# Layer-1 attention scores from f32 q and k held in 32-row lanes, their maxima turned in f32 and added to q, in place of bf16 parts stacked through DRAM

## The chip, the cores and the metric

The kernel runs on one core of one Trainium2 chip, as one program. The metric is the device time of one execution in microseconds (us); the median of three executions of the kernel before is 785.51 us (784.35 to 786.27). Five engines work in parallel, each through its own instructions in order: PE (matrix products), DVE (vector), ACT (scalar functions and copies), POOL (here memsets and indirect gathers) and SP (it issues DMA transfers). Engines wait for one another by semaphores. PE writes to PSUM banks of 512 f32 columns, from which DVE and ACT read.

## What is computed

Two transformer layers over x of 4 batches x 256 tokens x 256 values, each layer LayerNorm, attention, a gate, and `x + s * g`:

```
xn = layernorm(x)
s  = attention0(xn)      # 32 heads of 8 values, 8 k/v heads, biases, no mask
g  = silu(experts(xn))   # W_up, W_down, 45 keys, top 8 of 64 pairs, 8 heads x 8 experts a token:
                         # gathered rows of down_embed and up_embed
x  = x + s * g
xn = layernorm(x)
s  = attention1(xn):
       q = (xn @ Wq)                       # 16 heads of 16
       k, v = split(xn @ Wkv)              # 4 heads of 16, q head h reads k head h % 4
       scores = q k^T / sqrt(16) + slope[h] * (key - query)   for key <= query, else -inf
       out = softmax(scores) @ v, then @ Wo + bo
g  = silu(int8_linear(xn))                 # q = round(xn / scale), q @ weight^T, scales, bias, f16
x  = x + s * g
```

Layer 0 feeds layer 1 within a batch; batches are independent.

## The kernel before, in words

A batch is 256 tokens, two tiles of 128 rows. What a batch does is cut into stages, each with a number of calls: `stage:b.n` is call n of batch b. The order of the calls on each engine is written out by hand in four tables, `PE_PLAN` (L76), `ACT_PLAN` (L122), `DVE_PLAN` (L156) and `SP_PLAN` (L196); four batches are interleaved in them. A call waits by semaphores for what it reads and for what it overwrites; a wait at the head of an engine holds up all calls behind it.

**The experts of layer 0** run over 64 groups g (16 a batch), each for one head of 128 tokens. POOL gathers 8 x 128 table rows of 384 values a group (L551, one indirect DMA per expert, 512 in all) into one of `RING` = 4 slots. DVE's `dots:g` multiplies the first 128 values of each row with the token's h (L1204), ACT's `tanh` and DVE's `zs` (L1214) make the factors, ACT's `diag` (L1049) writes three of them on diagonals, DVE's `acc:g` (L1229) sums five of the eight rows and PE's `add:g` (L831) sums the other three into the PSUM bank `experts`. POOL may gather group g when `add` and `acc` of group g-4 are done. After the eight groups of a tile DVE's `mix` (L1290, L1292) joins both sums and frees `experts` for the next tile; add:16, add:24, ... add:48 are the first adds after a mix.

**Attention 0 and, before the change, attention 1** get f32 accuracy from bf16 products: DVE's `split` (L1174 to L1176) cuts q and k into three bf16 parts, SP stores the parts to DRAM (`store_parts`, L490, L491) and loads them back stacked (`load_stack`, L503, L506), so that one product of up to 128 rows holds all pairs of parts (`stackq`, `stackk`). `max0` and `max1` (L683; L696, L698, L701) are scores with the queries in rows, of which DVE takes the negated row maxima; `nm0`, `nm1` split the maxima in three and bring them as rows to `stackq` (layer 0) or `slopeq` (layer 1: transposed at L711, copied by ACT, placed by a DMA). `sc0` and `sc1` (L734; L743, L744, L746) are the scores again with the keys in rows, less the maxima; ACT takes their exponent (L997) and `pv0`, `pv1` (L766, L777) multiply with v. In layer 1 a unit of `max1` or `sc1` is four heads of one k head (`quad_of`): 12 units a batch, of which 8 lie on the diagonal and take a mask product (below, near units) and 4 do not (far). The ALiBi term is a product of its own, `slopeq` x `slopek`, of 512 bf16 columns. Then `ctx1` transposes the context, `over1` on DVE divides by the sums, `flip1` and `proj1` (L571, L807, L811) transpose and multiply with Wo. `turnq` and `quant` (L674) are the int8 linear layer.

**qkv1** (L629 to L641) makes q (256 columns twice), k and v from `x1T`, whose transposes (L571) ACT copies out; ACT copies q and k twice, in f32 and in bf16. PSUM banks of the stages' results are three, used in turn (`TURNS` = 3), in the order in which PE's plan names them. `warm:0.0` and `warm:0.1` (L839), at the end of PE's plan, are products whose results nobody reads.

**The start.** POOL clears the upper rows of `stackk` and `stackq`, then v0 and v1, and writes ones into v (L533 to L540). DVE normalises batch 0 (L1067 to L1080), PE transposes it (L571, with `ident`) and so on, until the first 128 lookups of batch 0 are there and POOL gathers.

A record of the trace is one pass of PE: a plain f32 product leaves two records (x2), a bf16 product or a transposition one. `order` listings, below, count products.

## Time and profile before

| | before |
|---|---|
| median of 3 executions | 785.51 us (784.35 to 786.27) |
| the profiled execution | 787.66 us |
| its span in the trace | 785.8 us |
| granted TensorE clock, mean | 0.823 |
| PE busy | 528.0 us (67%) |
| DVE busy | 592.4 us (75%) |
| ACT busy | 255.8 us (33%) |
| POOL busy | 514.9 us (66%), of which 512 gathers 505.0 us |

The span is from the first instruction to the last in the trace; 1.9 us of the profiled execution lie around it. POOL's gathers take 986 ns each with 0.30 us between two of them. PE's clock is 2.4 GHz where the trace shows 1.00 and 1.2 GHz where it shows 0.5; a value in between is a stretch with both. "Idle" at an instruction is the time in which its engine did nothing before it, and the arrow names who ended that.

### The profile page before, as it was taken

How to read it: one execution, taken by the hardware profiler on the slowest of the kernel's cores; microseconds unless marked ns; L12 is line 12 of the kernel's file. 1: busy time of each engine (PE TensorE's matmuls, PEld its weight loads, DVE VectorE, ACT ScalarE, POOL GpSimd, SP SyncE). 2: the span in 40 equal slices, each digit the busy share in tenths (PEclk: the TensorE clock that was granted, in tenths of full speed). 3: DMA queues.
4: the chain of work that ended last, by engine and by line, in shares of the span. 5: the costliest groups of instructions: out<-in, count | busy, mean ns of one | idle time of the engine just before them, and what ended most of it. 6: DMA issues, size and time to landing. Idle time of an engine off the chain costs nothing.

```text
span 785.8 us, 9193 instructions
## 1 busy us (share of the span) xinstructions
PE 528.0 (67%) x2241; PEld 291.8 (37%) x2258; DVE 592.4 (75%) x2700; ACT 255.8 (33%) x648; POOL 514.9 (66%) x522
## 2 busy tenths in 40 slices
PE   2810466486794567797758558956356996979786
PEld 2600254232373235334336235324233443354432
DVE  4487977797874987799779788869799875775351
ACT  1600151144541112463424114623111473425032
POOL 5077777777775777777777777777777777760000
PEclk9955787788986666899868767978777998989898
DMA  8157565555575555955765555596865559550400
GB/s 292 38 165 220 168 173 155 154 156 155 151 223 162 156 156 165 232 153 153 210 198 159 156 158 160 158 237 186 210 191 153 154 153 256 157 142 1 106 2 15
DMA packets 47765, 125.49 MB, mean 160 GB/s; under 512 B 10715, under 2 KB 20507, under 8 KB 46654
## 3 DMA queue, kind: packets, MB, share of 16 engines
q0 software_dynamic: 32768, 100.70, 45.3%
q1 hardware_dynamic: 14342, 23.90, 10.9%
q10 hardware_dynamic: 600, 0.30, 0.2%
q8 instruction: 18, 0.29, 0.2%
q14 instruction: 37, 0.30, 0.1%
HBM read 119.58 MB, written 4.98 MB: 159 GB/s over the span
## 4 chain that ended last, share of the span: by engine, by line
POOL 50%; issue 18%; PE 13%; DVE 12%; DMA 5%; ACT 1%; POOLq 0%; ACTq 0%; DVEq 0%
POOL rows L551 50%; DMA rows<-experts_table,idx 5%; PE experts L831 3%; DVE hot L1204 3%; DVE acc L1229 2%; PE outs L777 1%; PE experts L839 1%; PE turn L586 1%; PE turn L811 1%; DVE nmax L1245 1%; DVE nmax L1237 1%; PE scores L743 1%; DVE bestp L1129 1%; DVE var L1072 1%; PE turn L807 1%
## 5 line engine op out<-in xcount | busy, mean ns | idle before, releaser
L551 POOL DMA_INDIRECT rows<-experts_table,idx x512 | 505.0, 986 | 188.7 <-issue 151.4
L1204 DVE CUSTOM_DVE_ANT_0 hot<-rows,h 128x128 f32<-128x128 f32 x512 | 114.6, 287 | 108.6 <-DMA rows<-experts_table,idx 108.4
L831 PE MATMUL experts<-rows,diag 128*128 128x256 f32 x384 | 132.4, 497 | 45.4 <-ACT diag L1049 38.2
L683 PE MATMUL turn<-stackk,stackq 125*128 125x256 bf16 x256 | 58.4, 344 | 105.8 <-DVE nmax L1237 52.1
L1229 DVE SCALAR_TENSOR_TENSOR acc<-rows,zs,acc 128x256 f32<-128x256 f32 x304 | 125.7, 478 | 0.9 <-issue 0.3
L831 PEld LDWEIGHTS experts<-rows,diag 128*128 128x128 f32 x384 | 93.3, 254 | 76.5 <-ACT diag L1049 47.0
L997 ACT ACTIVATE probs<-scores 128x512 f32<-128x512 f32 x176 | 97.3, 594 | 59.6 <-PE scores L734 31.1
L1043 ACT ACTIVATE zt<-za 128x8 f32<-128x8 f32 x64 | 13.4, 209 | 259.5 <-DVE za L1208 259.3
L1049 ACT ACTIVATE diag<-ident,zs 128x128 f32<-128x128 f32 x192 | 63.1, 394 | 68.3 <-DVE zs L1214 63.8
L1237 DVE TENSOR_REDUCE nmax<-turn 128x2 f32<-128x512 f32 x128 | 82.2, 682 | 1.8 <-PE turn L683 1.7
L683 PEld LDWEIGHTS turn<-stackk,stackq 125*128 125x128 bf16 x256 | 21.7, 111 | 143.8 <-DVE nmax L1237 78.5
L766 PE MATMUL outs<-probs,v 128*32 128x512 f32 x256 | 68.0, 624 | 7.6 <-ACT probs L997 7.2
L734 PE MATMUL scores<-stackq,stackk 128*128 128x512 bf16 x113 | 38.2, 402 | 8.8 <-DMA stackq<-nmaxT 4.1
L1204 DVE DVE_READ_ACCUMULATOR2_ANT z<- 128x1 f32 x512 | 41.4, 81 | 0.0
L586 PE MATMUL turn<-xnT,wup 128*128 128x256 f32 x128 | 36.0, 443 | 3.1 <-DVE nmax L1237 2.3
L586 PEld LDWEIGHTS turn<-xnT,wup 128*128 128x128 f32 x128 | 28.6, 228 | 9.9 <-DVE nmax L1237 1.9
L734 PEld LDWEIGHTS scores<-stackq,stackk 128*128 128x128 bf16 x128 | 9.9, 101 | 56.8 <-ACT probs L997 31.8
L696 PE MATMUL turn<-slopeq,slopek 128*128 128x512 bf16 x48 | 19.5, 407 | 15.1 <-DMA stackk<-scratchk 9.9
L777 PE MATMUL outs<-probs,v 128*32 128x512 f32 x96 | 25.4, 619 | 1.7 <-ACT probs L997 1.7
L1245 DVE TENSOR_REDUCE nmax<-turn 128x4 f32<-128x512 f32 x32 | 20.9, 683 | 5.5 <-PE turn L701 5.5
L615 PE MATMUL turn<-simw,h2T 128*128 128x360 f32 x32 | 16.9, 656 | 10.5 <-ACT sims L865 9.0
L571 PE MATMUL turn<-ident,th_up 128*128 128x128 f32 x16 | 4.4, 430 | 27.5 <-DVE th_up L1080 16.8
(156 smaller groups left out, 751.5 us busy)
## 6 DMA issues: line engine op xcount, KB each, us to landing
rows<-experts_table,idx POOLq DMA_INDIRECT x512, 3.2
stackq<-scratchq SPq DMA_DIRECT2D x20, 384.0 KB
scratchq<-parts SPq DMA_DIRECT2D x8, 384.0 KB, 3.2
stackk<-scratchk SPq DMA_DIRECT2D x20, 96.0 KB
xnext<-x SPq DMA_DIRECT2D x4, 256.0 KB, 3.2
wup<-w_wup SPq DMA_DIRECT2D x1, 1024.0 KB, 4.9
slopeq<-c_slopeq SPq DMA_DIRECT2D x1, 1024.0 KB, 5.2
xres<-x SPq DMA_DIRECT2D x4, 256.0 KB, 3.4
```

Source lines behind the costliest of these rows:

```text
L551: nc.gpsimd.indirect_dma_start(rows[:, slot, c, :], None, tab, bass.IndirectOffsetOnAxis(ap=idx[:, b % 2, t, TOP * h + c:TOP * h + c + 1], ...
L586: ins = mm(ps[:, a * S:(a + 1) * S], wup[:, c, (2 * j + a) * P:(2 * j + a + 1) * P], xnT[:, c, :], start=(c == 0), stop=(c == DC - 1))
L683: ins = mm(ps[:, t * S:(t + 1) * S], stackq[0][r, m, t * P:(t + 1) * P], stackk[0][r, m // QUAD, :], start=True, stop=True)
L734: mm(scores[:, score_bank(0, UNITS[0] * b + m), :], stackk[0][:, u, kc * P:(kc + 1) * P], stackq[0][:, hd:hd + 2, :], start=True, stop=Tru ...
L766: ins = mm(outs[WIN * strip:WIN * (strip + 1), :], v0[:, kc, lead:lead + WIN], probs[:, nth[0, UNITS[0] * b + AT_ONCE * n + i] % PROBS, :] ...
L777: ins = mm(outs[WIN * u:WIN * (u + 1), :], v1[:, tk, WIN * u:WIN * (u + 1)], probs[:, nth[1, UNITS[1] * b + AT_ONCE * n + i] % PROBS, :], ...
L831: ins = mm(experts[:, s // FH, :], diag[:, g % 2, k, :], rows[:, g % RING, k, PRIV:ROW], start=(s % FH == 0 and k == 0), stop=(s % FH == F ...
L997: fn(probs[:, at % PROBS, :], scores[:, at % SCORES, :], ACT.Exp).then_inc(exp_done[layer], 1)
L1049: ins = fn(diag[:, g % 2, k, :], ident[:, :], ACT.Copy, scale=zs[:, g % FACTORS, k:k + 1])
L1204: ins = v.tensor_tensor_reduce(out=zjunk[:, k, :], in0=rows[:, slot, k, 0:PRIV], in1=h2[:, b % 2, t, :], scale=1.0, scalar=0.0, op0=ALU.mu ...
L1229: ins = v.scalar_tensor_tensor(total, row, factor, total, ALU.mult, ALU.add)
L1237: v.tensor_reduce(nmax[0][:, :, m], ps[:, :].rearrange("p (t k) -> p t k", k=S), AX.X, ALU.max, negate=True)\
```

## The change

Layer 1 keeps q and k in f32. The 128 rows of `q1` (128 x 4 x 256) and `k1` (128 x 256) are four lanes of 32 rows, one for each k head: row 0 of a lane is 1 in k, row 1 holds the slope in q and the key position in k, rows 2 to 17 the head's 16 values (slope x query is the same for all keys of a query and is left out). `wq1` and `wk1` are padded to this layout by the host. Part by part:

- `qkv1` is three calls with a bank each: k and v (with a bf16 product `rowk` x `posk` that writes ones and positions into k, L654), then q in two halves, each 4 f32 products of 256 columns (L661): 8 for q where there were 4. ACT copies k and v, and q with the slopes as bias; no bf16 copies.
- `max1` is, for a near unit, a bf16 mask product (L700) and four f32 products of one lane (32 rows) with 128 columns each (L703); a far unit has the four alone. Before: bf16 512 columns, 4 x 128 columns, and the mask's 512.
- `sc1` is the mask product (near, L751) and one f32 product of a lane with 512 columns (L752). Before: bf16 512 columns twice, and the mask's 512.
- The maxima of `max1` go to row 0 of each lane in `nwide` (128 x 2 x 4 x 128 f32). `nm1:b.t` on PE transposes four 128 x 128 blocks of it into a bank (L723), and the new `lift1:b.t` on DVE adds the bank to a half of `q1`. Gone: `split_maxima` of layer 1, ACT's copy and DMA.
- Gone with the parts: `split1` on DVE, `store1` and `stack1` on SP (8 transfers a batch), the loads of `slopeq` (1 MB) and `slopek`, and both calls of `warm`.
- POOL clears v0, v1 and `nwide` first and the stacks after `xn0_ready`, that is when DVE has normalised batch 0; SP's `ones:0.0` waits for that.
- The tables are written anew. The plan's calls around the last batch of layer 0 and at the end are among those that moved.

```diff
-    qkv0:3.0 max1:1.5 ctx0:2.0 add:0.46 flip0:2.0 add:0.47 proj0:2.0 max1:1.6 max1:1.7 max0:3.0 max0:3.1 add:0.48 add:0.49
...
+    sc1:1.4 sc1:1.5 sc1:1.6 max0:3.0 max0:3.1 max0:3.2 sc1:1.7 pv1:1.2 sc1:1.8 pv1:1.3 max0:3.3 max0:3.4 max0:3.5 sc1:1.9
+    add:0.48 add:0.49 max0:3.6 max0:3.7 max0:3.8 pv1:1.4 add:0.50 max0:3.9 sc1:1.10 max0:3.10 sc1:1.11 max0:3.11 pv1:1.5
...
-        slopeq = sb("slopeq", [P, H1, S], BF16)
-        slopek = sb("slopek", [P, 2, S], BF16)
+        slopes = sb("slopes", [P, QUAD])
+        rowk = sb("rowk", [P, P], BF16)
+        posk = sb("posk", [P, S], BF16)
...
+        q1 = sb("q1", [P, QUAD, S])
+        k1 = sb("k1", [P, S])
...
+        nwide = sb("nwide", [P, TT, QUAD, P])
+        nlanes = nwide[:, :, :, :].rearrange("p t j (u r) -> p t j u r", r=LANE)
...
-            nc.gpsimd.memset(stackk[0][CLEARED_FROM:P, :, :], 0.0)
-            nc.gpsimd.memset(stackq[0][CLEARED_FROM:P, :, :], 0.0).then_inc(cleared, 1)
-            pool.wait_ge(cleared, 1)
             nc.gpsimd.memset(full(v0), 0.0)
             nc.gpsimd.memset(full(v1), 0.0).then_inc(cleared, 1)
+            pool.wait_ge(cleared, 1)
+            nc.gpsimd.memset(v0one, 1.0)
+            nc.gpsimd.memset(v1one, 1.0)
+            nc.gpsimd.memset(full(nwide), 0.0).then_inc(cleared, 1)
             pool.wait_ge(cleared, 2)
-            nc.gpsimd.memset(v0one, 1.0)
-            nc.gpsimd.memset(v1one, 1.0).then_inc(cleared, 1)
+            pool.wait_ge(xn0_ready, 1)
+            nc.gpsimd.memset(stackk[CLEARED_FROM:P, :, :], 0.0)
+            nc.gpsimd.memset(stackq[CLEARED_FROM:P, :, :], 0.0).then_inc(stacks_cleared, 1)
...
+            def qkv1(b, n):
+
+                if b == 0 and n == 0:
                     pe.wait_ge(late_in, LATE_IN)
                 pe.wait_ge(drained["norm1"], b + 1)
-                qkv("qkv1", b, wq1, wk1, wv1, None, x1T)
+                ps = bank("qkv1", 3 * b + n)
+                if n == 0:
+                    mm(ps[:, 0:S], full(rowk), full(posk), start=True, stop=False)
+                    for c in range(DC):
+                        mm(ps[:, 0:S], wk1[:, c, :], x1T[:, c, :], start=False, stop=(c == DC - 1))
+                    ins = values_of(ps, wv1, x1T, None)
+                else:
+                    for a in range(2):
+                        for c in range(DC):
+                            ins = mm(ps[:, a * S:(a + 1) * S], wq1[:, c, 2 * (n - 1) + a, :], x1T[:, c, :],
+                                     start=(c == 0), stop=(c == DC - 1))
+                ins.then_inc(filled["qkv1"], 1)
...
             def max1(b, m):
                 if m == 0:
                     if b == 0:
-                        pe.wait_ge(late_in, LATE_IN)
                         pe.wait_ge(halves, 2)
-                    pe.wait_ge(stack_in[1], STACK_IN[1] * (b + 1))
+                    pe.wait_ge(drained["qkv1"], 3 * (b + 1))
                 u, tq, tk = quad_of(m)
                 ps, q, k = bank("max1", UNITS[1] * b + m), slice(tq * P, (tq + 1) * P), slice(tk * P, (tk + 1) * P)
-                each = ps[:, :].rearrange("p (j k) -> p j k", k=P)
-                mm(each, slopek[:, 0, q], slopeq[:, QUAD * u:QUAD * (u + 1), k], start=True, stop=False)
+                near = tq == tk
+                if near:
+                    mm(ps[:, :].rearrange("p (j k) -> p j k", k=P), full(identb),
+                       maskb[:, :].unsqueeze(1).broadcast_to([P, QUAD, P]), start=True, stop=False)
                 for j in range(QUAD):
-                    ins = mm(ps[:, j * P:(j + 1) * P], stackq[1][:, QUAD * u + j, q], stackk[1][:, u, k], start=False,
-                             stop=tq != tk and j == QUAD - 1)
-                if tq == tk:
-                    ins = mm(each, full(identb), maskb[:, :].unsqueeze(1).broadcast_to([P, QUAD, P]), start=False, stop=True)
+                    ins = mm(ps[:, j * P:(j + 1) * P], q1[lane(u), j, q], k1[lane(u), k], start=not near,
+                             stop=not near or j == QUAD - 1)
                 ins.then_inc(filled["max1"], 1)
...
+            def nm1(b, t):
+                if t == 0:
+                    pe.wait_ge(drained["max1"], UNITS[1] * b + QUADS[1])
+                else:
+                    pe.wait_ge(nmax1_ready, b + 1)
+                ps = bank("nm1", TT * b + t)
+                for j in range(QUAD):
+                    ins = tr(ps[:, j * P:(j + 1) * P], nwide[:, t, j, :], full(ident))
+                ins.then_inc(filled["nm1"], 1)
...
             def sc1(b, m):
-                if m == 0:
-                    pe.wait_ge(nmax_in[1], 16 * (b + 1))
                 u, tq, tk = quad_of(m)
-                q, k, hd = slice(tq * P, (tq + 1) * P), slice(tk * P, (tk + 1) * P), slice(QUAD * u, QUAD * (u + 1))
+                if m in (0, QUADS[1]):
+                    pe.wait_ge(drained["nm1"], TT * b + tq + 1)
+                q, k = slice(tq * P, (tq + 1) * P), slice(tk * P, (tk + 1) * P)
                 to = scores[:, score_bank(1, UNITS[1] * b + m), :].rearrange("p (j q) -> p j q", q=P)
-                mm(to, slopek[:, 1, k], slopeq[:, hd, q], start=True, stop=False)
-                ins = mm(to, stackk[1][:, u, k], stackq[1][:, hd, q], start=False, stop=tq != tk)
-                if tq == tk:
-                    ins = mm(to, full(identb), maskT[:, :].unsqueeze(1).broadcast_to([P, QUAD, P]), start=False, stop=True)
-                ins.then_inc(scores_ready[1], 1)
+                near = tq == tk
+                if near:
+                    mm(to, full(identb), maskT[:, :].unsqueeze(1).broadcast_to([P, QUAD, P]), start=True, stop=False)
+                mm(to, k1[lane(u), k], q1[lane(u), :, q], start=not near, stop=True).then_inc(scores_ready[1], 1)
...
+            def qkv1(b, n):
+                ps = bank("qkv1", 3 * b + n)
+                if n == 0:
+                    wait_from(act, scores_ready[1], UNITS[1] * b)
+                    wait_from(act, pv_done[1], PRODUCTS[1] * b)
+                    fn(full(k1), ps[:, 0:S], ACT.Copy)
+                    ins = fn(v1at, ps[:, S:S + TT * VD].rearrange("p (t g d) -> p t g d", t=TT, d=HD1), ACT.Copy)
+                else:
+                    if b == 0:
+                        act.wait_ge(late_in, LATE_IN)
+                    for a in range(2):
+                        j = 2 * (n - 1) + a
+                        ins = fn(q1[:, j, :], ps[:, a * S:(a + 1) * S], ACT.Identity, bias=slopes[:, j:j + 1], scale=HD1 ** -0.5)
+                ins.then_inc(drained["qkv1"], 1)
...
             def max1(b, m):
                 u, tq, tk = quad_of(m)
+                wait_from(dve, filled["nm1"], TT * (b - 1) + tq + 1 if b else 0)
                 dve.wait_ge(filled["max1"], UNITS[1] * b + m + 1)
-                ps, hd = turn[turns.bank["max1", UNITS[1] * b + m]], slice(QUAD * u, QUAD * (u + 1))
-                to = nmaxd[:, hd] if tk else nmax[1][:, tq, hd]
+                ps = turn[turns.bank["max1", UNITS[1] * b + m]]
+                to = nmaxd[:, :, u] if tk else nlanes[:, tq, :, u, 0]
...
             def nm1(b, _):
-                split_maxima(1, b)
+                dve.wait_ge(drained["max1"], UNITS[1] * (b + 1))
+                v.tensor_tensor(nlanes[:, 1, :, :, 0], nlanes[:, 1, :, :, 0], full(nmaxd), ALU.min).then_inc(nmax1_ready, 1)
+
+            def lift1(b, t):
+
+                dve.wait_ge(filled["nm1"], TT * b + t + 1)
+                dve.wait_ge(filled["max1"], UNITS[1] * b + (QUADS[1] if t == 0 else UNITS[1]))
+                ps = turn[turns.bank["nm1", TT * b + t]]
+                to = q1[:, :, t * P:(t + 1) * P]
+                v.tensor_tensor(to, to, ps[:, :].rearrange("p (j q) -> p j q", q=P), ALU.add).then_inc(drained["nm1"], 1)
```

The tables' two pieces above are of PE's plan, where before `add:48` follows the first two `max0` of batch 3, and after it comes after six of them. In the order of the instructions as built, three places:

**POOL from its first own instruction to the gathers**, before and after (v is v0, then v1; the names with few columns write the ones):

```order
L533 MEMSET stackk 64x2048
L534 MEMSET stackq 64x8192
L536 MEMSET v 128x576
L537 MEMSET v 128x256
L539 MEMSET v 128x2x8
L540 MEMSET v 128x8
L551 DMA rows<-experts_table,idx 128x384 x512
```

```order
L522 MEMSET v 128x576
L523 MEMSET v 128x256
L525 MEMSET v 128x2x8
L526 MEMSET v 128x8
L527 MEMSET nwide 128x1024
L530 MEMSET stackk 64x2048
L531 MEMSET stackq 64x8192
L542 DMA rows<-experts_table,idx 128x384 x512
```

The two stack memsets moved from the head to a place behind v, `nwide` and the wait for the normalised batch 0, just ahead of the gathers.

**PE around add:48 and add:49 (L831 before, L836 after), where batch 3 of layer 0 meets batch 1 of layer 1.** L683 and L687 are `max0:3`, two products a head; L811 projects; L751 and L752 are `sc1:1`, L782 `pv1:1`; L696 to L701 `max1:1`. Before, then after:

```order
L811 MATMUL turn<-wo,headsT 128x256 x4
L696 MATMUL turn<-slopeq,slopek 128x512
L698 MATMUL turn<-stackk,stackq 128x128 x4
L701 MATMUL turn<-maskb,identb 128x512
L696 MATMUL turn<-slopeq,slopek 128x512
L698 MATMUL turn<-stackk,stackq 128x128 x4
L701 MATMUL turn<-maskb,identb 128x512
L683 MATMUL turn<-stackk,stackq 128x256 x4
L831 MATMUL experts<-rows,diag 128x256 x6
L683 MATMUL turn<-stackk,stackq 128x256 x12
L831 MATMUL experts<-rows,diag 128x256 x3
```

```order
L752 MATMUL scores<-q,k 128x512 x2
L751 MATMUL scores<-maskT,identb 128x512
L752 MATMUL scores<-q,k 128x512
L687 MATMUL turn<-stackk,stackq 128x256 x6
L751 MATMUL scores<-maskT,identb 128x512
L752 MATMUL scores<-q,k 128x512
L782 MATMUL outs<-probs,v 32x512 x2
L752 MATMUL scores<-q,k 128x512
L782 MATMUL outs<-probs,v 32x512 x2
L687 MATMUL turn<-stackk,stackq 128x256 x6
L752 MATMUL scores<-q,k 128x512
L836 MATMUL experts<-rows,diag 128x256 x6
```

Where two heads of `max0:3` and two units of `max1:1` stood ahead of add:48, there are now `sc1:1.4` to `sc1:1.9`, `max0:3.0` to `3.5` and `pv1:1.2`, `1.3`; `max1:1` is over by then. The first product of batch 3's stack is L683 before and L687 after.

**PE from the last layer norm to the first scores of batch 3 of layer 1.** Before, then after:

```order
L571 MATMUL turn<-ident,qf 128x128 x4
L777 MATMUL outs<-probs,v 32x512 x2
L629 MATMUL turn<-headsT,wq 128x256 x4
L634 MATMUL turn<-headsT,wk 128x256 x2
L641 MATMUL turn<-wv,headsT 128x64 x4
L788 MATMUL turn<-ident,ctxT 128x128 x8
L571 MATMUL turn<-ident,heads 128x128 x4
L807 MATMUL turn<-bo,ident 128x512
L811 MATMUL turn<-wo,headsT 128x256 x4
L839 MATMUL experts<-stackk,identb 128x512 x28
L696 MATMUL turn<-slopeq,slopek 128x512
L698 MATMUL turn<-stackk,stackq 128x128 x4
```

```order
L836 MATMUL experts<-rows,diag 128x256 x3
L812 MATMUL turn<-bo,ident 128x512
L816 MATMUL turn<-wo,headsT 128x256 x4
L562 MATMUL turn<-ident,qf 128x128 x4
L654 MATMUL turn<-posk,rowk 128x256
L656 MATMUL turn<-headsT,wk 128x256 x2
L624 MATMUL turn<-wv,headsT 128x64 x4
L661 MATMUL turn<-headsT,wq 128x256 x8
L562 MATMUL turn<-identb,qb 128x128 x4
L700 MATMUL turn<-maskb,identb 128x512
L703 MATMUL turn<-k,q 128x128 x4
```

The projection of batch 2 (L807, L811; after L812, L816) moved ahead of the transposes of batch 3's normalised rows (L571 and L562 from `qf`), the warm-up products (L839) are gone, and `max1:3` (after L700, L703) follows `qkv1:3` and `turnq:3` directly.

## Rows read from the trace of the kernel before

**Rows 1.** The page: the chain that ended last, shares of the span.

```profile
POOL 50%; issue 18%; PE 13%; DVE 12%; DMA 5%; ACT 1%; POOLq 0%; ACTq 0%; DVEq 0%
```

**Rows 2.** Who waited for whom, POOL: us in total, times, longest.

```profile
POOL rows L551 <- PE experts L831: 8.1, 9, 5.7
```

**Rows 3.** Order of time to 40 us: start, us, instruction, [idle before <-releaser].

```profile
2.48 6.92 POOL L534 MEMSET stackq<- 64x8192 bf16 x1
...
4.39 5.04 DVE L1072 TENSOR_SCALAR var<-mv 128x2 f32<-128x2 f32 x1
...
8.16 0.21 ACT L870 ACTIVATE bup_half<-bup 128x8 f32<-128x8 f32 x1 [6.13 <-DMA bup<-w_bup]
...
9.46 0.59 POOL L536 MEMSET v<- 128x576 f32 x1
...
10.36 0.18 DVE L1074 TENSOR_SCALAR rstd<-bits 128x2 int32<-128x2 uint32 x1
...
13.22 1.09 PE L571 MATMUL turn<-ident,th_up 128*128 128x128 f32 x4 [13.22 <-DVE th_up L1080]
...
38.15 1.09 POOL L551 DMA_INDIRECT rows<-experts_table,idx  x1 [27.63 <-DVE idx L1160]
```

**Rows 4.** Order of time around group 20, DVE and POOL.

```profile
244.02 0.29 DVE L1204 CUSTOM_DVE_ANT_0 hot<-rows,h 128x128 f32<-128x128 f32 x1 [9.20 <-DMA rows<-experts_table,idx]
...
250.06 1.14 POOL L551 DMA_INDIRECT rows<-experts_table,idx  x1 [5.66 <-PE experts L831]
```

**Rows 5.** Order of time, 499 to 581 us, PE, DVE and POOL.

```profile
499.08 1.46 PE L831 MATMUL experts<-rows,diag 128*128 128x256 f32 x6
...
540.16 1.00 PE L641 MATMUL turn<-wv,xnT 128*128 128x64 f32 x8
...
545.63 0.96 DVE L1176 TENSOR_TENSOR parts<-hot,parts 128x768 bf16<-128x768 f32 x1
...
570.24 1.04 PE L683 MATMUL turn<-stackk,stackq 125*128 125x256 bf16 x4 [11.60 <-DMA stackk<-scratchk]
...
574.94 5.18 PE L831 MATMUL experts<-rows,diag 128*128 128x256 f32 x12 [3.67 <-DVE mixed L1292]
...
580.26 1.04 POOL L551 DMA_INDIRECT rows<-experts_table,idx  x1 [0.30 <-PE experts L831]
```

**Rows 6.** Windows: length, busy of PE PEld DVE ACT POOL, clock, DMA.

```profile
500.00:541.00 41.00, 30.91 (x140) 14.97 (x140) 31.65 (x155) 15.06 (x37) 31.49 (x32) 0.88 0.75 203
...
664.00:701.00 37.00, 29.78 (x159) 15.33 (x162) 29.33 (x122) 15.90 (x38) 28.20 (x29) 0.92 0.60 179
...
730.00:737.00 7.00, 5.65 (x13) 3.73 (x14) 1.11 (x3) 0.60 (x1) 0.00 (x0) 0.52 0.74 165
```

**Rows 7.** DVE in order of time, then the chain after the last gather.

```profile
719.37 0.73 DVE L1080 TENSOR_SCALAR qf<-x,mv,rstd 128x256 f32<-128x256 f32 x2
...
724.15 0.86 PE turn L634 x4
...
737.45 5.99 PE experts L839 x27
...
743.44 0.22 PE turn L696
...
744.13 1.35 DVE nmax L1245 x2
...
762.41 0.98 PE outs L777 x4
...
763.39 0.32 PE scores L743
...
772.97 0.61 ACT ctxT L1010
```

**Rows 8.** Order of time, PE: an f32 product of 128 columns, then of 64.

```profile
34.76 0.38 PE L636 MATMUL turn<-bv,ident 128*128 128x128 f32 x2
...
34.98 1.00 PE L641 MATMUL turn<-wv,xnT 128*128 128x64 f32 x8
```

464 lines of the change are left out of this document (200 added, 264 removed).

## The prediction

> **What bounds the kernel now.** First the page's chain of what ended last: half of the span is POOL's gathers, and the 18% "issue" is mostly the 0.30 us between two of them [rows 1]. So from 38.15 us, when the first gather starts, to 706 us the time is 512 gathers, and a change elsewhere counts there only by what it lets POOL wait. The view of who waited for whom says how much that is: 8.1 us behind PE's adds in nine waits, the longest 5.7 [rows 2]. The rest of the span is a start, in which POOL waits 27.6 us for the first indices [rows 3], and a tail after the last gather, where PE, DVE and ACT take turns. I read three stretches closely.
>
> At the start DVE's `var`, two columns, takes 5.04 us where the like `rstd` takes 0.18, and it ends when POOL's 6.92 us memset of `stackq` ends; PE's first transposes wait for DVE at 13.22 [rows 3]. Before group 20 POOL idles 5.66 us behind PE's add, which follows a mix on DVE that stands behind rows awaited until 244.02 [rows 4]. Around 540 to 580 layer 0's last batch is stacked: `qkv0:3` ends at 541.0 on PE, the split on DVE ends at 546.6, the first `max0:3` starts at 570.24 when the stack has landed, add:48 and add:49 follow at 574.94, and POOL goes on at 580.26 with no more than its normal gap [rows 5]. There the adds' lead over POOL is 580.26 - 577.5, the end of add:48, the latter 2.6 us (half of 5.18) after its start: 2.8 us of slack.
>
> **Part 1, the start: -5.0.** The stack memsets leave the head of POOL, and v with 576 columns costs 0.59 [rows 3], so `nwide` with 1024 costs 1.0 by columns: POOL is done with what is left at about 3, ahead of DVE's 4.39. DVE then gets back 4.9 on `var` and 0.7 on `bits`, and the first transposes start at 7.6. PE next needs other loads: the last small one of those for `up`, `bup`, is there by 8.16 [rows 3], and the transposes and their copy (13.22 to 15.0) end at 9.4, after that. I take 5.0 of 5.6, leaving 0.6 for weights that may now be late. Bounds: 0, if another cause held DVE, and 5.6. The memsets of the stacks now run beside PE's `up`, 8.7 us before `split0:0`. They are ahead of the gathers on POOL, but those wait for indices much longer.
>
> **Prices of the lane products.** The trace has no product of 32 rows. What it has, by columns, at full clock: an f32 product of 128 columns 0.22 (34.76 to 34.98) [rows 8], of 256 columns 0.43 (two in 0.86), thus of 512 0.86; a bf16 one of 512 columns 0.22 [rows 7]. I take the lane products at these, the nearest rows there are. For a change between a lane and the whole array I take the nearest rows, `pv`, whose products go to strips of 32 columns: four records cost 0.98 where 4 x 0.22 = 0.88 is the columns' time, and the scores after them 0.32 instead of 0.22 [rows 7]: 0.10 + 0.12, about 0.2 for a round trip. Bounds: 0 and 0.4. Only near units switch (mask, whole array, then lanes). So a near unit of `max1` is 0.22 + 4 x 0.22 + 0.2 = 1.3, a far one 0.9; `sc1` near 0.22 + 0.86 + 0.2 = 1.3, far 0.9. A batch: `max1` 8 x 1.32 + 4 x 0.9 = 14.2, `sc1` 13.9. Before, by the 0.22 a record set, these were 7.0 and 6.9. `qkv1` adds four products of q (1.7), less the leaner rest; `nm1` adds six transposes, 1. PE gains some 17 us of work a batch, and POOL-bound time pays for it only where PE's slack ends.
>
> A record here lasts 0.38 where the next starts 0.22 after it (34.76 to 34.98 [rows 8]); were PE emptied at each change, both ways would cost 2 x 0.16 = 0.32 instead of 0.2. That is rival (c) below. The Trainium skill, TensorEngine Tiling (Array Packing), section Key Properties, says that changing the tiling mode drains TensorE; that speaks against this change, which makes 16 such round trips a batch, and by it the sum would be 783.9 and not 780.7. The strips of `pv`, at 0.2, agree only in part.
>
> **Part 2, group 20: 0.** The new order has the same calls (dots:18 ahead of the mix) on DVE, so the stall of 5.66 stays [rows 4].
>
> **Part 3, batch 3's stack: +3.5.** This is where slack was least. From 500 to 541 PE was busy 30.9 of 41 us at clock 0.88 [rows 6]. The new plan puts between the end of add:42 and that of `qkv0:3`: 11 pairs of `pv` (10.8), 20 `sc0` with their switches (5.5), all 12 `max1:1` (14.2), `nm1` (1.3), 3 adds (3.9), `sc1:1.0` to `1.3` (5.2), `turnq` (0.3), `qkv0:3` (3.9): 45 us. add:42 starts at 499.08 [rows 5] and ends at 500.4; 2 us later now, as `qkv1:1` with more products stands right ahead. 502.4 + 45.3 = 547.7 (all in the old time scale, the -5.0 apart) for 541.0. DVE's split follows at once now, without the 2.9 us of other work ahead of it, and ends at 551.7 for 546.6. Store and stack took 23.6 from there (546.6 to 570.24), so `max0:3` starts at 575.3. Ahead of add:48 stand now six `max0`, three units of `sc1` and two pairs of `pv`, 6.4 us against 4.7 before. add:48 ends at 575.3 + 6.4 + 2.6 = 584.3, against 580.3 where POOL would go on: 3.5 to 4, of which later groups give back nothing, since POOL has no slack of its own. Bounds: 0, if PE kept the old pace, to 8, where the work is 0.1 dearer a lane product.
>
> **Part 4, the end: -3.3.** From 664 to 701 PE was busy 29.8 of 37 us [rows 6]; with `max1:2`, `sc1:2` and more it is full in groups 58 to 62, and I put add:62 and `ctx1` about 3 us late. DVE's last norm, which needs the last mix, ends at 722.1 for 720.1 [rows 7]: +2.0, as the last projections now stand ahead in PE's plan but off this path. From there to the end before took 65.7. Now: transposes and copy 1.8; `qkv1:3` with eight q products 5.7; last copy 0.75; `max1`, `sc1` and the rest of the block 36.8, which is 14.2 + 13.9, three pairs of `pv` twice (5.9), `nm1` 1.3, `quant` 0.6, and 0.9 of waiting for a lift. DVE needs 0.68 a unit (1.35 for two [rows 7]), under PE's 0.9 and 1.3. The last part from ctxT at 772.97 [rows 7] to 785.8 stays, 12.85. PE idles 3.8 us during the norm; before, an idle stretch of that length at 726.7 to 730.6 was followed by 7 us at clock 0.52 [rows 6], the lower of its two levels. This time the 7 us hold `qkv1` and the first `max1`: I put 2.5 on it, below the 3.5 that half the clock costs on constant work. Sum 60.4, for 65.7: -5.3, and +2.0 makes -3.3. What goes is the DVE split, store and stack, which 27 warm-up records (5.99 us of 737.45 on [rows 7]) filled in. Bounds: -8, if switches and clock cost nothing and the norm ends on time; +4, at dearer products and a full half-clock price.
>
> **Sum.** 785.8 - 5.0 + 3.5 - 3.3 = 781.0 of span, 782.9 for the profiled execution (787.66 before), which lay 2.15 above the median. Median 785.51 - 4.8 = 780.7. A measurement of this kernel can tell from no change about 0.3%, 2.4 us.
>
> **The rivals.** (a) Lanes are cheap: no cost of switching, PE keeps pace, no stall at 52, the end on time. For it: rows of a product that are unused cost nothing elsewhere. Then -5.0, 0 and -7.7: 772.8. (b) Slower: the weights of a lane do not load behind the product before. 48 products of `max1` a batch are 128 columns behind a new load each; at 0.32 for 0.22, each batch's `max1` costs 4.8 more in three places where PE is by then the bound: the stall at 52 becomes 8.3, the end +3, the tail +4.8: 780.7 + 12.6 = 793.3. For it: four products of 64 columns cost about 0.84 (1.00 less the last record's 0.16 over its spacing), 0.21 each and not 0.11 [rows 8]: new weights set their pace, and 128 columns only just cover them. Against it: they do cover them. It decides from 0.26 us a product, where 780.7 becomes 785.7. (c) Full drains: 0.32 a round trip, 16 in the tail (+1.9) and 11 in part 3 (+1.3): 783.9. (d) Half clock more often: each switch leaves idle pieces, and PE drops to 1.2 GHz as in 730 to 737 in one or two busy stretches; six us each of doubled work, half hidden: 786.5. (e) Neighbouring lanes side by side: products of two lanes overlap. Only far units stand next to a unit of another lane, which saves 1.8 in the tail and 1 in part 3: 777.5.
>
> On (e), the trace has no two products in different rows at one time. The Trainium skill, same page and section, says that tiles operate independently and can run in parallel; by it the whole of lanes back to back would overlap, which the plan offers only between far units.
>
> (f) The change does not do what it says at the start: DVE was held by something other than the memset, and 5.0 is not gained: 785.7.
>
> **How the numbers follow.** Forecast 780.7: 0.38. (a) 772.8: 0.20. (b) 793.3: 0.14. (c) 783.9: 0.08. (d) 786.5: 0.06. (e) 777.5: 0.06. (f) 785.7: 0.08. Low 771 takes in (a) with 2 us, high 790 takes in (c), (d), (f) and the lesser half of (b): about 0.8 within, with what lies beyond (a). Faster by over 2.4 us: the forecast's case, (a) and (e): 0.64. Slower by over 2.4: (b): 0.14. Within 2.4: (c), (d) and (f): 0.22.
>
> **What would show it.** Start: `var` at 0.2 us and the first gather at 33 to 33.5. Prices: `max1`'s f32 products 0.22 us apart, near units 1.3 in the block. Batch 3: `qkv0:3` ending about 1.7 later than before in absolute time (547.7 - 5.0), and POOL idle 3 to 4 us once at group 52; none if (a). End: norm's last row 60 us ahead of the end, and clock 0.5 for 7 us right behind it. I would be wrong if lane products take 0.26 us or more, if PE's backlog reaches the adds of other groups (add:24 to add:40 have some slack that I did not go through one by one), or if the start waits on a load instead.

## The result and the profile after

The changed kernel takes 807.76 us (median of 4, 806.58 to 813.05), the kernel before 785.26 in the same set; the ratio is 1.0287, 95% interval 1.0257 to 1.0316. The forecast was 780.7, in a range of 771 to 790: it was wrong, in sign too. The profiled execution took 806.58 with a span of 804.7 (before 787.66 and 785.8), so 18.9 us of span have to be found.

The start, answering [rows 3], from the timelines of DVE, PE and POOL after:

```profile
4.80 0.17 DVE L1058 TENSOR_SCALAR var<-mv 128x2 f32<-128x2 f32 x1
...
8.85 1.12 PE L562 MATMUL turn<-ident,th_up 128*128 128x128 f32 x4 [8.85 <-DMA bup<-w_bup]
...
34.05 1.09 POOL L542 DMA_INDIRECT rows<-experts_table,idx  x1 [17.35 <-DVE idx L1146]
```

DVE's `var` is fast, the first gather is 4.1 us earlier, and the limit is now the load of `bup`. The gather stream, from who waited for whom on POOL, and the middle, from the timelines, answering [rows 2, 5]:

```profile
POOL rows L542 <- PE experts L836: 16.9, 7, 9.2
```

```profile
565.88 1.03 PE L687 MATMUL turn<-stackk,stackq 125*128 125x256 bf16 x4 [7.96 <-DMA stackk<-scratchk]
568.40 0.61 PE L687 MATMUL turn<-stackk,stackq 125*128 125x256 bf16 x2 [1.49 <-ACT proj L858]
568.89 0.61 PE L751 MATMUL scores<-maskT,identb 128*128 128x512 bf16 x1
569.42 2.07 PE L752 MATMUL scores<-q,k 32*128 32x512 f32 x2
571.43 1.92 PE L782 MATMUL outs<-probs,v 128*32 128x512 f32 x4
...
579.92 2.86 PE L836 MATMUL experts<-rows,diag 128*128 128x256 f32 x12
...
581.76 0.98 POOL L542 DMA_INDIRECT rows<-experts_table,idx  x1 [9.16 <-PE experts L836]
```

Every PE row from 568.40 to 577 lasts about twice what its like lasts elsewhere: `pv` 1.92 for 1.05, a lane product with 512 columns 2.07 for 1.12. The stream from first to last gather takes 668.7 us for 665.1: 9.7 more of waits for PE and DVE, 5.8 less of gathers (975 ns for 986).

The tail, windows of the kernel after: length, busy time of PE, PEld (TensorE's weight loads), DVE, ACT, POOL, granted clock, DMA share and GB/s. It answers [rows 6, 7]:

```profile
718.00:740.00 22.00, 16.51 (x75) 12.85 (x74) 11.56 (x35) 3.73 (x9) 0.00 (x0) 0.84 0.04 13
740.00:760.00 20.00, 20.00 (x83) 14.35 (x82) 6.23 (x9) 1.19 (x2) 0.00 (x0) 0.50 0.00 0
760.00:770.00 10.00, 10.00 (x28) 3.64 (x27) 2.32 (x5) 1.79 (x3) 0.00 (x0) 0.50 0.01 2
770.00:780.00 10.00, 9.22 (x23) 2.40 (x20) 1.51 (x3) 3.39 (x6) 0.00 (x0) 0.67 0.00 0
780.00:790.00 10.00, 10.00 (x16) 1.94 (x16) 0.00 (x0) 1.79 (x3) 0.00 (x0) 0.50 0.00 1
```

This is the finding. From 740 to 770 PE is busy in 30.00 of 30.00 us, and its granted clock is 0.50 throughout, the lower of its two levels. Before, 27 whole-array products and the block after them ran at 1.00, though PE was busy for less of the time:

```profile
744.00:773.00 29.00, 25.97 (x150) 10.62 (x149) 12.22 (x27) 9.78 (x18) 0.00 (x0) 1.00 0.01 2
```

PE's timeline after shows the fall, and it is not at an idle stretch:

```profile
737.43 0.39 PE L700 MATMUL turn<-maskb,identb 128*128 128x512 bf16 x1
737.75 1.15 PE L703 MATMUL turn<-k,q 32*128 32x128 f32 x8
738.83 0.39 PE L700 MATMUL turn<-maskb,identb 128*128 128x512 bf16 x1
739.15 1.61 PE L703 MATMUL turn<-k,q 32*128 32x128 f32 x8
740.70 0.61 PE L700 MATMUL turn<-maskb,identb 128*128 128x512 bf16 x1
741.23 4.11 PE L703 MATMUL turn<-k,q 32*128 32x128 f32 x24
745.27 1.11 PE L723 MATMUL turn<-ident,nwide 128*128 128x128 f32 x4
746.18 0.63 PE L700 MATMUL turn<-maskb,identb 128*128 128x512 bf16 x1
746.75 2.07 PE L703 MATMUL turn<-k,q 32*128 32x128 f32 x8
748.75 0.61 PE L700 MATMUL turn<-maskb,identb 128*128 128x512 bf16 x1
```

Four products of a lane (8 records) cost 1.08 (737.75 to 738.83) before the fall and 2.00 (746.75 to 748.75) after it. PE idled nowhere between 736.02, where it had waited 0.71 us for ACT, and the fall at about 740. The clock came back once, at about 770, behind the int8 products, eight records of `pv1` and four transpositions, and fell again within 4 us in lane products of `sc1`:

```profile
770.38 0.66 PE L723 MATMUL turn<-ident,nwide 128*128 128x128 f32 x4
771.82 1.13 PE L752 MATMUL scores<-q,k 32*128 32x512 f32 x4 [0.78 <-DVE q L1248]
...
775.16 2.07 PE L752 MATMUL scores<-q,k 32*128 32x512 f32 x2
```

**Where the 18.9 us are**, by spans: first gather -4.1; stream +3.6; last gather to the end of the last norm (725.04 for 720.10) +5.4; from there to the end 79.7 for 65.7, +14.0. I call the stretch from the first `max1:3` (736.0) to the last `pv1:3` (793.6) the block below; in the tables of the experiments it is counted from the first lane product.

### The profile page after: what moved, and what is told of

Read it like the earlier page. It is cut to its first block, busy times and chain, and to the rows that moved or that the text cites. A ratio compares the mean times of both kernels' runs of the same rounds, so it can differ in the third digit from the quotient of the medians.

```text
span 804.7 us, 9495 instructions
## 1 busy us (share of the span) xinstructions
PE 590.4 (73%) x2396; PEld 328.5 (41%) x2412; DVE 582.4 (72%) x2680; ACT 253.9 (32%) x648; POOL 509.9 (63%) x523
## 4 chain that ended last, share of the span: by engine, by line
POOL 50%; PE 23%; issue 19%; DVE 4%; DMA 3%; ACT 1%; SPq 0%; POOLq 0%; DVEq 0%; ACTq 0%
POOL rows L542 50%; PE scores L752 4%; PE turn L703 4%; PE experts L836 3%; PE outs L782 2%; PE outs L771 2%; DMA rows<-experts_table,idx 2%; PE turn L577 1%; DVE hot L1184 1%; PE scores L740 1%; DMA bup<-w_bup 1%; PE scores L751 1%; DVE nmax L1217 1%; PE turn L700 1%; DMA stackq<-nmaxT 1%
## 5 line engine op out<-in xcount | busy, mean ns | idle before, releaser
L542 POOL DMA_INDIRECT rows<-experts_table,idx x512 | 499.2, 975 | 187.8 <-issue 151.1
L836 PE MATMUL experts<-rows,diag 128*128 128x256 f32 x384 | 126.0, 477 | 42.3 <-ACT diag L1035 30.5
L687 PE MATMUL turn<-stackk,stackq 125*128 125x256 bf16 x256 | 59.4, 348 | 100.7 <-DVE nmax L1217 57.6
L836 PEld LDWEIGHTS experts<-rows,diag 128*128 128x128 f32 x384 | 87.1, 240 | 75.0 <-ACT diag L1035 39.5
L687 PEld LDWEIGHTS turn<-stackk,stackq 125*128 125x128 bf16 x256 | 22.0, 112 | 141.0 <-DVE nmax L1217 84.2
L771 PE MATMUL outs<-probs,v 128*32 128x512 f32 x256 | 65.2, 618 | 5.4 <-ACT probs L992 4.6
L752 PE MATMUL scores<-q,k 32*128 32x512 f32 x96 | 59.6, 763 | 2.9 <-DVE q L1248 2.9
L703 PE MATMUL turn<-k,q 32*128 32x128 f32 x384 | 59.2, 320 | 0.0
L703 PEld LDWEIGHTS turn<-k,q 32*128 32x128 f32 x384 | 50.9, 219 | 14.8 <-issue 13.9
L1226 DVE TENSOR_REDUCE nwide<-turn 128x4 f32<-128x512 f32 x32 | 21.4, 686 | 22.3 <-PE turn L703 22.3
L577 PEld LDWEIGHTS turn<-xnT,wup 128*128 128x128 f32 x128 | 29.5, 235 | 11.1 <-DVE heads L1262 4.0
L782 PE MATMUL outs<-probs,v 128*32 128x512 f32 x96 | 31.2, 812 | 0.4 <-ACT probs L992 0.4
```

Of the source, the lines that this page charges most:

```text
L542: nc.gpsimd.indirect_dma_start(rows[:, slot, c, :], None, tab, bass.IndirectOffsetOnAxis(ap=idx[:, b % 2, t, TOP * h + c:TOP * h + c + 1], ...
L577: ins = mm(ps[:, a * S:(a + 1) * S], wup[:, c, (2 * j + a) * P:(2 * j + a + 1) * P], xnT[:, c, :], start=(c == 0), stop=(c == DC - 1))
L687: ins = mm(ps[:, t * S:(t + 1) * S], stackq[r, m, t * P:(t + 1) * P], stackk[r, m // QUAD, :], start=True, stop=True)
L703: ins = mm(ps[:, j * P:(j + 1) * P], q1[lane(u), j, q], k1[lane(u), k], start=not near, stop=not near or j == QUAD - 1)
L752: mm(to, k1[lane(u), k], q1[lane(u), :, q], start=not near, stop=True).then_inc(scores_ready[1], 1)
L771: ins = mm(outs[WIN * strip:WIN * (strip + 1), :], v0[:, kc, lead:lead + WIN], probs[:, nth[0, UNITS[0] * b + AT_ONCE * n + i] % PROBS, :] ...
```

## The experiments

Two theories stood at the start. **A**: products of 32 rows do not hold PE's clock at 2.4 GHz, however busy PE is. **B**: the idle 4 us of PE in the last norm, with nothing to warm it up, set it back. With them **C**, lane products are dear in themselves, and **D**, changes between lanes and the whole array let the clock fall.

One thing has to be known to read the totals: on three of the chips the gather stream took some 200 us longer, for every kernel, the one before included (medians of 985 to 994 us); why is not known. Totals are used only where the kernel before takes 785 to 789; what comes after the last gather is comparable everywhere: the block of whole-array products took 32.7 us on each of five chips of both kinds.

| run | rows of products | block us | clock | total | ratio to before |
|---|---|---|---|---|---|
| changed kernel | 32 | 57.2 | 0.56 | 807.8 | 1.0287 (1.0257 to 1.0316) |
| e7_after_again | 32 | 59.6 | 0.53 | 808.3 | 1.0246 (1.0184 to 1.0308) |
| e1_rows128 | 128 | 32.7 | 1.00 | slow stream | |
| e2_rows64 | 64 | 35.9 | 1.00 | slow stream | |
| e4_fill2 | 32, filled | 62.3 | 0.78 | slow stream | |
| e6_kzero | 128 | 32.7 | 1.00 | 773.0 | 0.9783 (0.9745 to 0.9821) |
| e8_max_lanes | max1 32, sc1 128 | 43.8 | 0.77 | 792.1 | 1.0046 (1.0003 to 1.0088) |
| e9_sc_lanes | max1 128, sc1 32 | 43.9 | 0.77 | 790.1 | 0.9992 (0.9946 to 1.0037) |
| e11_kzero_add48 | 128 | 32.7 | 1.00 | 775.6 | 0.9852 (0.9794 to 0.9909) |
| e12_rows64_kept, e12b | 64 | 46.4, 46.4 | 0.76 | slow stream | |
| e13_full_last, e13b | last batch 128 | 32.7, 32.7 | 1.00 | slow stream | |
| e14_after_oldstart, e14b | 32 | 57.4, 59.9 | 0.56, 0.52 | slow stream | |

The block of 32-row products comes in two lengths, 57.2 and 57.4 or 59.6 and 59.9. In e7_after_again the four transpositions at 773.64 still ran at half clock (1.12 us for 0.66): the short return of the clock that the result shows at 770 did not come there.

**Rows alone.** The row ranges of the products change, and on the host the ones in row 0 of k are kept in one lane only:

```diff
-                    ins = mm(ps[:, j * P:(j + 1) * P], q1[lane(u), j, q], k1[lane(u), k], start=not near,
+                    ins = mm(ps[:, j * P:(j + 1) * P], q1[0:P, j, q], k1[0:P, k], start=not near,
...
-                mm(to, k1[lane(u), k], q1[lane(u), :, q], start=not near, stop=True).then_inc(scores_ready[1], 1)
+                mm(to, k1[0:P, k], q1[0:P, :, q], start=not near, stop=True).then_inc(scores_ready[1], 1)
```

> The changed kernel, with the f32 products of max1 and sc1 over all 128 rows of q1 and k1 instead of one 32-row lane: same count, columns, places and waits; the scores are then sums over four k heads, so the output is another (row 0 of k holds its 1 in one lane only, which keeps the numbers finite). Theory A (products of 32 rows do not hold PE's clock at 2.4 GHz, though PE is busy): the block from the first max1:3 to the last pv1:3, 57.6 us in the changed kernel at a clock of mostly 0.50, takes about 36 at 1.00, and the stretch before add:48 some 5 less: 780 to 786. Rival B (the clock falls because PE idles 4 us during the last norm and nothing warms it up): only the first 7 us are slow, and they stay: within 3 us of the changed kernel's 807.8, less 0.1 us for each of the 32 changes of rows a batch. Rival C (the lane products are simply dear): the spacing of products at clock 1.00 falls, e.g. 1.05 for an sc1 product to 0.86, and the time falls by 10 at most.

The total lies on a chip with a slow stream and says nothing. The block does: 32.7 us at 1.00 for 57.2 at 0.56, with the norm's idle stretch ahead as before. That is against B, and against C as the main cause: at clock 1.00 a lane unit costs 1.40 and a whole-array unit 1.11, which is 0.3 for each of 16 near units and not 24.5 for the block. From e1's PE timeline:

```profile
937.79 0.38 PE L700 MATMUL turn<-maskb,identb 128*128 128x512 bf16 x1
938.01 1.05 PE L703 MATMUL turn<-k,q 128*128 128x128 f32 x8
938.90 0.38 PE L700 MATMUL turn<-maskb,identb 128*128 128x512 bf16 x1
```

The same with `64 * (u // 2):64 * (u // 2) + 64` for the rows:

> As the one with 128 rows, but products over 64 rows (two lanes). The changes between full array and half array stay, as do all counts. Theory A as a matter of degree (more rows, more clock): in between or, if 64 rows are enough, 783 to 790 with the clock back at 1.00 in the block. If it is the change of rows itself that lowers the clock (rival D): no better than the changed kernel, 805 to 810.

Block 35.9 at 1.00. It has all the changes of rows, so D falls. The 3.2 us over 32.7 are their price less what neighbouring units of different rows save by overlapping (24 records in 2.53 for 2.68), and the changed kernel's own rows at full clock give the price alone: mask to lane 0.32 for 0.22, lane to mask 1.08 for 0.89 (937.79 to 938.90, less the mask's 0.22). About 0.3 a round trip.

**Fill between the lane products.** After each unit of the last batch:

```diff
+                if b == B - 1:
+                    pe.wait_ge(mixed_ready, TT * B)
+                    for _ in range(2):
+                        mm(experts[:, :, :], full(identb), stackk[:, 0:TT, :], start=True, stop=True)
```

> The changed kernel with two bf16 products of 512 columns over the whole array (0.22 us each at full clock) added behind each of the 24 units of max1 and sc1 of the last batch, results unread: 48 products, 10.4 us of work at full clock. Theory A: whole-array work between the lane products brings the clock up; at 1.00 the block takes 36 + 10.4 = 47 instead of 57.6, so some 797. Rival B or C: clock as before or price as before, 10 to 20 us slower than 807.8.

A miss, though a telling one. Windows of this run, columns as above:

```profile
980.00:996.00 16.00, 16.00 (x78) 7.29 (x77) 3.97 (x8) 3.39 (x6) 0.00 (x0) 1.00 0.00 1
996.00:1012.00 16.00, 14.66 (x25) 3.07 (x24) 1.29 (x2) 3.21 (x6) 0.00 (x0) 0.61 0.00 0
1012.00:1027.00 15.00, 15.00 (x27) 3.06 (x28) 0.00 (x0) 2.39 (x4) 0.00 (x0) 0.51 0.00 1
```

With the fill the first half holds 1.00. After the 1.34 us in which PE waits for the second lift, the same kind of mixture (`sc1` lanes and fill, PE busy) runs at full clock for some 2 us more, falls, and stays at 0.5 to the end. So in this run a mixture that held the clock up did not bring it back, and this much fill is no remedy: the block is 62.3. That the wait set off the fall is not shown; e1 and e2 waited 1.1 us in the same place and stayed at 1.00.

**Whole-array products, the result kept.** `k1` gets four copies, copy u holding lane u and zeros elsewhere; then q needs no lanes, and nothing is added on PE:

```diff
-        k1 = sb("k1", [P, S])
+        k1 = sb("k1", [P, KV1, S])
...
+            pool.wait_ge(stacks_cleared, 1)
+            nc.gpsimd.memset(full(k1), 0.0).then_inc(stacks_cleared, 1)
...
-                    ins = mm(ps[:, j * P:(j + 1) * P], q1[lane(u), j, q], k1[lane(u), k], start=not near,
+                    ins = mm(ps[:, j * P:(j + 1) * P], q1[:, j, q], k1[:, u, k], start=not near,
...
-                mm(to, k1[lane(u), k], q1[lane(u), :, q], start=not near, stop=True).then_inc(scores_ready[1], 1)
+                mm(to, k1[:, u, k], q1[:, :, q], start=not near, stop=True).then_inc(scores_ready[1], 1)
...
-                    fn(full(k1), ps[:, 0:S], ACT.Copy)
+                    if b == 0:
+                        act.wait_ge(stacks_cleared, 2)
+                    for u in range(KV1):
+                        fn(k1[lane(u), u, :], ps[lane(u), 0:S], ACT.Copy)
```

> The changed kernel with products over all 128 rows, and the result kept: k1 has four copies, each with one lane filled and zeros elsewhere (cleared once on POOL behind the stacks; ACT copies k in four pieces of 32 rows, about 1.1 us more a batch), so q1 needs no lanes in max1 and sc1. Theory A (32-row products let PE's clock fall): block of max1:3 to pv1:3 33 us at clock 1.00 for 57.2 in the changed kernel, tail about 23 shorter; before add:48 no half-clock lane work, stall at group 52 of 9.2 down to about 4. On a chip where the changed kernel takes 807.8 that is 778 to 782, under the kernel before (785.3). Rival C (lane products dear in themselves): 797 or more.

> The changed kernel itself, for the chip of this set. Both theories: 807 to 810 if the kernel before takes 785 here, with the block at clock 0.56 and 57 us.

On one chip: 772.95 against 808.3 for the changed kernel and 788.55 for the one before. It beats both, the latter by 2.2%, and lies below the 778 to 782 expected. Its block, in two windows:

```profile
726.00:742.00 16.00, 16.00 (x118) 13.99 (x118) 8.21 (x12) 2.09 (x4) 0.00 (x0) 1.00 0.00 1
742.00:759.00 17.00, 15.72 (x57) 5.28 (x54) 3.05 (x6) 7.24 (x13) 0.00 (x0) 1.00 0.01 1
```

Between the spans of the two profiled executions (812.8 and 771.6) lie 41.2 us: block 26.9, what follows it 1.0, last gather to block 5.1 (PE's backlog at groups 60 to 63: add:63 starts 22.8 after its first gather for 16.4), last gather itself 8.3. At group 52 POOL waits 3.71 here, and 9.87 in the changed kernel on this chip (9.16 in its first run). So rows alone also cost in the gather stream, not only in the block. But part of that stretch is at half clock here too, with whole-array products, behind PE's wait:

```profile
566.62 0.61 PE L689 MATMUL turn<-stackk,stackq 125*128 125x256 bf16 x2 [2.48 <-ACT proj L860]
567.11 0.61 PE L753 MATMUL scores<-maskT,identb 128*128 128x512 bf16 x1
567.51 1.91 PE L754 MATMUL scores<-q,k 128*128 128x512 f32 x2
...
572.79 1.05 PE L784 MATMUL outs<-probs,v 128*32 128x512 f32 x4
```

There it is over by 572.8, some 6 us behind the wait; in the changed kernel it lasted to about 579, some 10 us.

**One half each.** e8 keeps the lanes in `max1` alone, e9 in `sc1` alone:

```diff
-                    ins = mm(ps[:, j * P:(j + 1) * P], q1[:, j, q], k1[:, u, k], start=not near,
+                    ins = mm(ps[:, j * P:(j + 1) * P], q1[lane(u), j, q], k1[lane(u), u, k], start=not near,
```

> As the one with four copies of k, but max1 alone on 32-row lanes; sc1 over all rows. Theory A: the stretch of max1:3 (736 to 768 in the changed kernel) falls to 0.50 and the one of sc1:3 after it runs at 1.00: about half of the 24 us of the block lost, 790 to 796. If it were only the long sc1 products: as with full rows, 778 to 783.

> Four copies of k, max1 over all rows, sc1 alone on 32-row lanes (the mirror image of the run with max1 alone on lanes, which took 792.1 for 773.0 and 808.3, block 43.8 us at clock 0.77). Theory A: the block's first half at 1.00, sc1's half mostly at 0.50, so again about half of the loss: 788 to 793, block 40 to 46 us. Rival (only max1's many small products do it): 773 to 776.

Both lose about half, in mirror image. In e8 the stretch of `max1` falls to half clock, the first whole-array `sc1` among it too (1.91 us at 750.68), and the stretch of `sc1` alone is at 1.00; in e9 it is the other way round. One row of either kind from each:

```profile
744.72 2.07 PE L705 MATMUL turn<-k,q 32*128 32x128 f32 x8
...
774.11 1.02 PE L754 MATMUL scores<-q,k 128*128 128x512 f32 x2
```

```profile
737.07 1.05 PE L705 MATMUL turn<-k,q 128*128 128x128 f32 x8
...
759.82 2.07 PE L754 MATMUL scores<-q,k 32*128 32x512 f32 x2
```

The clock follows the rows of the products that make up a stretch: counts and columns are the same in both. (e9's executions spread from 779 to 794, more than those of any other run off the slow streams.)

**32 rows in the kernel before.** Its stacked products cut to `0:32` in both places:

```diff
-                ins = mm(to, stackk[1][:, u, k], stackq[1][:, hd, q], start=False, stop=tq != tk)
+                ins = mm(to, stackk[1][0:32, u, k], stackq[1][0:32, hd, q], start=False, stop=tq != tk)
```

> The kernel before with the stacked products of layer 1 (max1's four of 128 columns, sc1's one of 512) cut to rows 0 to 31 of the stack; the slope and mask products over the whole array stay, as do all columns, transfers and waits. The output is another. Theory A with a share: in each unit a third to a half of the time is now 32-row work, two thirds whole array. If any such share suffices to lower the clock, the block from 743 on falls to 0.5 (+10 to +20); if whole-array work holds it up, clock 0.95 to 1.00 and the time only grows by the changes of rows, at 0.2 to 0.3 each for 24 units in the tail: +5 to +7. I expect the latter, 791 to 796 beside 785 to 788.

798.1 beside 786.75, ratio 1.0149 (1.0094 to 1.0204): more than expected. Windows of its tail:

```profile
755.00:765.00 10.00, 9.09 (x38) 3.88 (x39) 4.99 (x12) 1.57 (x3) 0.00 (x0) 0.58 0.00 0
765.00:775.00 10.00, 10.00 (x39) 2.73 (x37) 0.00 (x0) 4.81 (x8) 0.00 (x0) 1.00 0.01 4
```

With two thirds of whole-array work in the near units the clock is mostly at 1.00. It dips once, from 753 on, 2 us behind a wait of 1.69 us for DVE, and is back at 1.00 by 764, behind seven of the whole-array products that fill PE's time there. The kernel before waited 2.21 us in the same place (748.70) and stayed at 1.00. So a share of whole-array work can hold the clock; how large it must be is not settled.

**Half the rows, again, and the parts of the loss.** e12 is e6 with 64 rows, e13 is e6 with `slice(0, P) if b == B - 1 else lane(u)` for the rows, e14 the changed kernel with POOL's memsets in the old order.

> Four copies of k, products over 64 rows (the lane and its neighbour's zeros), result kept. On another chip 64 rows kept the clock at 1.00 in the block, 35.9 us for 32.7 with 128 rows and 57.2 with 32. Theory A (rows in use count, and half is enough): block 36, total 3 to 5 above the 773.0 of whole-array products: 776 to 778. If half the rows held the clock by chance on that chip only: 785 or more.

> Four copies of k, whole-array products in max1 and sc1 of the last batch alone, 32-row lanes in batches 0 to 2. Theory: the tail's block gives back its 25 to 27 us, what is lost earlier stays: 5 at group 52 and 3 to 6 of backlog at groups 60 to 63, so 782 to 785, against 773.0 with all and 808.3 with none.

> The changed kernel with POOL's memsets in the old order (stacks first). Theory: first gather at 38 to 39 instead of 34; as POOL's stream is the bound up to group 52 and the stall there is set by PE and SP work that starts later too, the whole is 3 to 5 slower: 811 to 813. Rival: the later stalls absorb it, 807 to 809.

All fell on chips with slow streams, and again when repeated (the expectations of the repeats, e12b, e13b and e14b, say the same), so no total divides the loss. Medians on the first of the two chips: e12 1008.6, e13 1020.8, e14 1038.9, the kernel before 993.8. The blocks are in the table. e13 shows that the tail's block is healed by its own products alone. e12 stays at 1.00 through `max1`, then PE waits 1.14 us for the lift, and some 2 us later its `sc1` run at 0.50, where e2 in the same place, after 1.15 us, kept 1.00. Windows of e12, then of e2:

```profile
942.00:960.00 18.00, 18.00 (x118) 12.81 (x119) 8.37 (x13) 1.80 (x4) 0.00 (x0) 1.00 0.00 0
966.00:988.00 22.00, 22.00 (x33) 4.34 (x32) 0.00 (x0) 4.33 (x8) 0.00 (x0) 0.50 0.00 0
```

```profile
948.00:966.00 18.00, 18.00 (x118) 12.66 (x117) 8.61 (x13) 1.79 (x3) 0.00 (x0) 1.00 0.00 0
966.00:983.00 17.00, 15.85 (x54) 4.50 (x52) 2.46 (x6) 7.14 (x12) 0.00 (x0) 1.00 0.01 1
```

So 64 rows held the clock through `max1` in three runs, and over a short wait in one of the three. Whether chance decides, or the neighbour's zeros in e12 where e2 has values, is open. (Zeros in 96 of 128 rows did no harm in e6.) e14's start is as expected: with the stack memsets at POOL's head again, `var` takes 4.88 us and the first gather is at 39.0.

**The start.** The kernel before with POOL's new order alone, first on a slow-stream chip, then again:

> The kernel before with only the start of the change: POOL clears v0 and v1 first and the stacks once batch 0 is normalised; ones wait for that. Theory: var takes 0.2 us, first gather 4 us earlier (34.1 for 38.15, the limit being the load of bup at 8.85), and since POOL's stream is the bound, the whole gains 4: about 781.3. Rival: the slack before add:48 (2.8 us) and the group 20 stall take it back: 784 to 785.

> The kernel before with the new order of POOL's memsets alone, once more beside the changed kernel. First gather 4 us earlier. Theory: 781.3; rival: the slack of 2.8 us at group 52 and other waits take it back, 784 to 785.

Nothing gained (0.9992, 0.9957 to 1.0027), since the first gather was at 39.7, later than before. DVE's `var` was fast (0.17 us), so it was the memset that held it, but ACT now reached the copy of the int8 weights before the last of the late loads, 1 MB of `slopeq` among them, and stood in the way of `up`:

```profile
23.27 0.63 ACT L878 ACTIVATE w8b<-w 128x512 bf16<-128x512 int8 x1 [4.29 <-DMA maskT<-c_maskT]
```

e10 adds the change's order on ACT, which I had not seen in the tables:

```diff
-    init:0.0 norm0:0.0 init:0.1 up:0.0 up:0.1 up:0.2 init:0.2 up:0.3 fold:0.0
+    init:0.0 norm0:0.0 up:0.0 init:0.1 up:0.1 up:0.2 up:0.3 init:0.2 fold:0.0
```

> The kernel before with the new order of POOL's memsets and, on ACT, identb's copy one step and the copy of the int8 weights behind the last up:0, as the change has it. With POOL's order alone ACT stood 4.3 us at the int8 weights' copy until the last of the late loads (1 MB of slopeq among them) had come, and the first gather was at 39.7. Theory: first gather at 34 to 35, and the whole 3 to 4 us below the kernel before. Rival: the later stalls (group 20, add:48) stand at fixed places of the program and give none of it back or all: within 1 us of before.

First gather at 33.0, total 783.79 beside 786.75: ratio 0.9953 (0.9927 to 0.9979), 3.0 of the 5.2 us that the first gather is earlier. A gain at the start mostly reaches the end here, but it took the edits on both engines.

**add:48 earlier**, in e6, directly behind `max0:3.2`:

```diff
-max0:3.0 max0:3.1 max0:3.2 sc1:1.7 pv1:1.2 sc1:1.8 pv1:1.3 max0:3.3 max0:3.4 max0:3.5 sc1:1.9 add:0.48 add:0.49
+max0:3.0 max0:3.1 max0:3.2 add:0.48 add:0.49 sc1:1.7 pv1:1.2 sc1:1.8 pv1:1.3 max0:3.3 max0:3.4 max0:3.5 sc1:1.9
```

> Four copies of k, whole-array products, and in PE's plan add:48 and add:49 moved up, directly behind max0:3.2, ahead of sc1:1.7 to 1.9, two pairs of pv1 and max0:3.3 to 3.5. There PE spent 567.5 to 575.3 on these, and POOL idled 3.7 us at group 52. Theory: the adds run at 568 to 571, POOL does not wait, 3.5 us less: 769 to 770. Rival: DVE's mix of the tile before is later than that (it stands behind max0:3.2 on DVE), and half or more is not gained: 771 to 773.

Neither figure: 775.6, ratio 0.9852 (0.9794 to 0.9909), on another chip than e6, whose interval it overlaps, so that it is slower than e6 is not shown. The rival's reason is seen: PE now stands at the add until DVE's mix, POOL still waits 2.88 us at group 52 for 3.71, and what was put off comes later (from the start of the last gather to the block 31.6 for 28.0):

```profile
574.11 5.49 PE L838 MATMUL experts<-rows,diag 128*128 128x256 f32 x12 [6.20 <-DVE mixed L1281]
```

## Why the prediction was wrong, step by step

The four parts of the sum against the spans: forecast 781.0, measured 804.7. One of the rivals' sums is off by a little: (e) is 780.7 less 2.8, 777.9 and not 777.5.

**Part 1, the start, -5.0: -4.1 measured.** Right in mechanism: `var` took 0.17 us, and the order of the memsets alone switches it between 0.17 and about 5 in both kernels (e3b, e14), which rules out rival (f). `bup`, which I placed at 8.16 and so harmless, came at 8.85 and was the last. Its price depended on edits that I did not name (ACT's two copies, 1 MB less to load), as e3b and e10 show.

**Prices, at full clock: right.** A round trip costs 0.3 where I had 0.2 and the full drain of rival (c) 0.32, so (c) was the better of the two. The Trainium skill, TensorEngine Tiling (Array Packing), section Key Properties (a change of mode drains TensorE), agrees: 0.32 for 0.22 into a lane and 1.08 for 0.89 out of it.

**Part 2, group 20, 0.** Right: 6.2 for 5.7.

**Part 3, +3.5.** The stream grew by 3.6, but by two errors that cancel. The work up to `qkv0:3` was sized right (44.1 us from add:42's end at 494.1 to 538.2, for 45.3), store and stack 23.9 for 23.6, and the stack was there at 565.88, 4.4 before the forecast, 3.3 of it as add:42 was early. Then "6.4 us" between it and add:48 were 14.0. Of these 7.6 more, PE stood idle for 1.5, behind a copy of ACT's, and was busy for 12.6 at a clock of 0.52, some 6 more than at full clock. About half of the 6 belongs to the idle stretch before, which in e6 too was followed by half clock (9.7 of busy time between the same two points), and the rest to the lane products, which kept the clock down longer. The stall grew by 8.9 where I had up to 4.0: the adds ended 2.5 later than forecast, and POOL was there 2.4 earlier. Against that, gathers were 5.8 us shorter in sum, which I had not expected and did not test.

**Part 4, the end, -3.3: +19.4.** The failed step is one term: "`max1`, `sc1` and the rest of the block 36.8", at 0.22 a record. At full clock it was about right (35.9 in e2, with all the changes of rows). It took 57.6. The step that failed is to take the clock of rows of other shapes: I priced the half clock as something that idle time causes and work ends, 2.5 us behind the norm, since rows of before showed only that [rows 6]; rival (d) had the same idea. The runs show in its place that 32-row products themselves let the clock fall while PE is busy: with nothing but the rows changed the block is 32.7 at 1.00 (e1). The stretch from the norm's end to the block is 11.0 for my 10.75, the last part 11.1 for 12.85. The norm ended 22.3 us after the last gather for 16.9, +5.4 and not +2.0: the backlog of groups 60 to 63, where the adds start 23 to 30 us behind the first gather of their group, in e6 16 to 23 and before 17 to 19.

No rival held this. (b), the slower side, had the place right (lane products, three stretches) and the sign, with a wrong reason (weights) and a third of the loss. (e) was right in its mechanism: at half clock 8 records of one lane take 2.00 and 24 of three lanes in a row 4.04, 1.02 for each further lane and not 1.78, twice the 0.89 of full clock. The Trainium skill, TensorEngine Tiling (Array Packing), section Key Properties (tiles run in parallel), agrees: records of two lanes even start together, at 752.85 (L752 and L703). With two such places in `max1` and the like in `sc1` it is small beside the clock. The Trainium skill, TensorE: Matmul & The Clock Gate, section What's actually happening, says that the clock follows how busy TensorE has been. Read as busy time, this case speaks against it: 30.00 of 30.00 us busy at 0.50.

## What to carry to other kernels

Products on a quarter of TensorE's rows were not only no faster here than whole ones: stretches made of them ran at half the clock, and slowed whatever stood between them. If an operand is short of rows, spread it over all 128 with zeros on one side (here four copies of k, 1.1 us of copies a batch for 35 us). When a plan changes the shape of products, ask of each long stretch at which clock it will run, and do not take the clock from rows of other shapes.

## What the runs showed of the hardware

- The granted clock fell from 1.00 to 0.50 in the midst of busy 32-row products (between 739 and 741 us), with no idle time in the 3 us ahead, and stayed there for 30 us of busy time.
- Holding and regaining can differ: fill of 0.44 us of whole-array products a unit held 1.00 (e4), and did not bring it back once it had fallen, 2 us behind a wait of 1.3; 64 rows likewise in e12 and e12b, but not in e2.
- Products of lanes at different rows overlap when they follow one another: 1.02 us for each further four at half clock, where four whole-array ones take 0.89 at full clock, so 1.78 at half.
- A memset of 6.92 us on POOL held a two-column instruction of DVE for 4.9 to 5.0 us; with the memset later it took 0.17.
- Zeros count as rows: with three quarters of k's rows zero the block ran at 1.00.
- The block of whole-array products took 32.71 to 32.72 us in five profiled runs on five chips, whose gather streams differ by 200 us.
